# Products of the Fourier mode mixing moved from VectorE to GpSimd, with four buffers and another order of the data

## The reference, cut to what matters

```python
x = x + _L0_conv_ref(_gn(x), weight_re, weight_im, bias)
x = x + _L1_conv_ref(_gn(x), gamma, beta)

# _L0_conv_ref: 4 heads of 16 channels, the lowest 32 x 17 modes
x_freq = jnp.fft.rfft2(x, axes=(-2, -1))
xf = x_freq.reshape(B, 4, 16, fH, fW)
core = jnp.einsum('bhixy,hioxy->bhoxy', xf[:, :, :, :32, :17], weight)   # complex
out_freq = zeros.at[:, :, :, :32, :17].set(core)
x_out = jnp.fft.irfft2(out_freq, s=(H, W), axes=(-2, -1)) + bias
# _L1_conv_ref: a per-pixel normalization on the hyperboloid (arccosh, sqrt, a sum over channels)
```

## Time and profile before

| | |
|---|---|
| median of 3 runs | 4943.81 us (4943.03 to 4945.26) |
| span of the profiled execution | 4939.4 us |
| its own time | not given apart from the span; the median of the runs lies 4.4 us above the span |
| busy: PE, DVE, ACT, POOL | 77%, 69%, 45%, 30% |
| stage a, about | 0 to 1350 us |

### The profile page before, as it was taken

How to read it: one execution, slowest core, us unless ns; L and a number is a source line. 1 busy time by engine, 2 the same in 40 slices (tenths; PEclk the granted TensorE clock), 3 DMA queues, 4 the chain that set the end, 5 groups by cost and what they waited for, 6 DMA issues and landing times.

```text
span 4939.4 us, 72319 instructions
## 1 busy us (share of the span) xinstructions
PE 3805.1 (77%) x23619; PEld 2097.6 (42%) x23874; DVE 3399.5 (69%) x3499; ACT 2240.3 (45%) x3020; POOL 1460.1 (30%) x737
## 2 busy tenths in 40 slices
PE   7777777777144344433999999999999999999998
PEld 3444444444111011002555555555555555555554
DVE  2989889898863433343776677667767776676677
ACT  5555555455022233232554455445554554454544
POOL 0010110101100010001454444444444444444444
PEclk9988888898566677766999999999999999999999
DMA  9565756655099989982777777777777777777776
GB/s 367 192 251 188 258 198 229 228 193 213 14 381 357 364 342 363 351 345 81 224 235 219 227 239 221 224 223 241 224 222 224 237 227 224 227 234 224 223 244 217
DMA packets 288845, 1197.47 MB, mean 242 GB/s; under 512 B 30174, under 2 KB 46846, under 8 KB 205828
## 3 DMA queue, kind: packets, MB, share of 16 engines
q1 hardware_dynamic: 274740, 1151.85, 68.7%
q0 software_dynamic: 11600, 38.32, 2.1%
q10 hardware_dynamic: 2304, 4.20, 0.2%
HBM read 883.32 MB, written 310.94 MB: 242 GB/s over the span
## 4 chain that ended last, share of the span: by engine, by line
PE 50%; issue 3%; DMA 1%; DVE 0%; SPq 0%; POOL 0%; ACT 0%; POOLq 0%; ACTq 0%
PE c_p_u L1129 20%; PE c_p_z L1099 11%; PE c_p_t L1112 10%; PE c_p_p L1153 5%; PE c_p_g L1135 4%; DMA c_mv<-bmap 0%; POOL c_ot L1306 0%; ACT c_zc L1189 0%; DVE c_zc L1280 0%; DMA c_ys<-spec 0%; SPq L1070 0%; DMA c_x<-x 0%; DVE c_rt L1288 0%; SPq L1069 0%; PE c_p_z L1174 0%
## 5 line engine op out<-in xcount | busy, mean ns | idle before, releaser
L1306 POOL TENSOR_TENSOR c_ot<-c_s,c_u 128x1024 f32<-128x1024 f32 x512 | 1211.3, 2366 | 1411.6 <-DVE c_s L1259 1411.6
L1189 ACT ACTIVATE c_zc<-c_p_z 34x512 f32<-34x512 f32 x512 | 546.4, 1067 | 1316.0 <-PE c_p_z L1099 1261.5
L1250 DVE TENSOR_TENSOR c_u<-c_xt,c_p_u 128x1024 f32<-128x1024 f32 x512 | 625.3, 1221 | 745.0 <-PE c_p_u L1129 722.5
L1129 PE MATMUL c_p_u<-c_mv,c_zc 128*128 128x256 f32 x4096 | 1043.7, 399 | 76.5 <-issue 75.5
L1129 PEld LDWEIGHTS c_p_u<-c_mv,c_zc 128*128 128x128 f32 x4096 | 750.7, 193 | 590.1 <-issue 465.7
L650 PE MATMUL b_p_al<-b_xt,b_awc 128*32 128x512 f32 x2048 | 333.9, 791 | 502.6 <-ACT b_al_r L692 314.9
L1259 DVE SCALAR_TENSOR_TENSOR c_s<-c_u,keep_k,c_p_g 128x1024 f32<-128x1024 f32 x512 | 655.8, 1281 | 18.0
L1269 DVE TENSOR_TENSOR c_ot<-c_ot,c_p_p 128x1024 f32<-128x1024 f32 x512 | 621.4, 1214 | 1.8 <-POOL c_ot L1306 1.3
L1218 ACT ACTIVATE c_sq<-c_s,c_btcol 128x1024 f32<-128x1024 f32 x512 | 589.2, 1151 | 52.8 <-DVE c_s L1259 22.3
L1099 PEld LDWEIGHTS c_p_z<-c_idft_h,c_ys 128*34 128x34 f32 x8176 | 477.6, 113 | 224.7 <-issue 215.2
L1099 PE MATMUL c_p_z<-c_idft_h,c_ys 128*34 128x64 f32 x8176 | 559.6, 222 | 7.8 <-ACT c_zc L1189 7.8
(11 more groups left out here) (177 smaller groups left out, 3090.8 us busy)
## 6 DMA issues: line engine op xcount, KB each, us to landing
a_xt<-in_x SPq DMA_DIRECT2D x256, 1024.0 KB, 9.7
b_xt<-in_x SPq DMA_DIRECT2D x128, 2048.0 KB, 18.9
c_xt<-in_x SPq DMA_DIRECT2D x256, 1024.0 KB, 6.4
out<-c_ot SPq DMA_DIRECT2D x256, 1024.0 KB, 8.5
maps<-b_maps POOLq DMA_DIRECT2D x16, 768.0 KB, 14.9
c_rt<-maps SPq DMA_DIRECT2D x256, 48.0 KB
a_wm<-in_wmix SPq DMA_DIRECT2D x1, 8704.0 KB, 34.9
b_spt<-spec POOLq DMA_DIRECT2D x32, 272.0 KB, 23.4
```

The costliest lines, as they stand in the source:

```text
L1129: ins = nc.tensor.matmul(p_u[:, W * r:W * r + W], zc[ck % 2][:, (t % TCH) * ROWS + row], mv[t % 2][:, W * row:W * row + W], start=True, st ...
L1189: S.activation(zc[chunk_buffer][0:M2, :, 16 * part:16 * part + 16].rearrange("m h c -> m c h"), p_z[0:M2, :].rearrange("m (c h) -> m c h", ...
L1250: V.tensor_tensor(u[n][:], xt[t % 4][:, 1024 * n:1024 * n + 1024], p_u[:], ALU.add).then_inc(u_done, 1)
L1306: P.tensor_tensor(ot[t % 4][:, 1024 * n:1024 * n + 1024], s0[n][:], u[n][:], ALU.add).then_inc(v_done, 1)
```

## The change

GpSimd forms all the products of an image in `products(b)`: 16 of 128x1088, one for each output, into four buffers `prod` in turn. Each waits until the sum that last read its buffer is done (`y_sums`). `second_rstd(b-1)` and `store_stats(b-1)` stand behind the fourth product. VectorE's `mix(b, q)` keeps only the two reductions, each behind the semaphore of its product, and `mean_sum` is called behind the fourth `mix` of the next turn. `xh`, the weights and the products are laid out with ky outside and the 32 pairs (channel, real/imaginary part) innermost, so that a reduction reads neighbouring elements; `xh` is written with that permutation. The host lays the weights out in the same order.

```diff
+    NP = 4
-        xh = sb("xh", [128, CI, M2])
-        prod = [sb(f"prod{k}", [128, 2, CI * M2]) for k in range(2)]
+        xh = sb("xh", [128, KY, 2 * CI])
+        prod = [sb(f"prod{k}", [128, 2, CI * M2]) for k in range(NP)]
...
-            def mix(q, waited=None):
+            def mix(b, q, stored=None):
                 for o in (2 * q, 2 * q + 1):
-                    ch.inc(V.tensor_tensor(prod[o % 2][:], wm[:, o], xh[:].rearrange("p i m -> p (i m)").unsqueeze(1).to_broadcast((128, 2, CI * M2)), ALU.mult))
-                ch.wait()
-                for o in (2 * q, 2 * q + 1):
-                    if waited is not None and o == 0:
-                        dve.wait_ge(y_out, waited)
-                    ch.inc(V.tensor_reduce(y[:, o].rearrange("p (a k) -> p a k", a=2), prod[o % 2][:].rearrange("p a (n k) -> p a k n", k=KY), AX_X, ALU.add))
-                ch.wait()
+                    dve.wait_ge(prod_ready, b * CI + o + 1)
+                    if stored is not None and o == 0:
+                        dve.wait_ge(y_out, stored)
+                    V.tensor_reduce(y[:, o].rearrange("p (a k) -> p a k", a=2), prod[o % NP][:].rearrange("p a (k n) -> p a k n", k=KY), AX_X, ALU.add).then_inc(y_sums, 1)
             def finish(b):
+                dve.wait_ge(y_sums, b * CI + CI)
...
-                ch.inc(V.tensor_tensor(xh[:].rearrange("p (g i) m -> p g (i m)", i=2), xk[:].rearrange("p (g i) m -> p g (i m)", i=2),
-                                       row(22, 8).unsqueeze(2).to_broadcast((128, 8, 2 * M2)), ALU.mult))
+                ch.inc(V.tensor_tensor(xh[:].rearrange("p k (g j) -> p g j k", j=4), xk[:].rearrange("p i m -> p (i m)").rearrange("p (g j k) -> p g j k", j=4, k=KY),
+                                       row(22, 8).unsqueeze(2).unsqueeze(3).to_broadcast((128, 8, 4, KY)), ALU.mult))
...
-                dcs = pair(xh[:, :, 0])
-                ch.step(V.tensor_tensor(dcs, dcs, row(7, 8).unsqueeze(2).to_broadcast((128, 8, 2)), ALU.add))
-                if not is_at(b, 0):
-                    mean_sum(b - 1)
+                dcs = pair(xh[:, 0, 0::2])
+                V.tensor_tensor(dcs, dcs, row(7, 8).unsqueeze(2).to_broadcast((128, 8, 2)), ALU.add).then_inc(xh_ready, 1)
+                dve.wait_ge(xh_ready, b + 1)
...
-                    neg = wm[:, :, 0].rearrange("p o (i r k) -> p o i r k", r=2, k=KY)[:, :, :, 1]
+                    neg = wm[:, :, 0].rearrange("p o (n r) -> p o n r", r=2)[:, :, :, 1]
...
-                    mix(q, None if is_at(b, 1) or q else (b - 1) * 16)
+                    mix(b - 1, q, None if is_at(b, 1) or q else (b - 1) * 16)
+                    if q == 3 and not is_at(b, 1):
+                        mean_sum(b - 2)
...
+            def products(b):
+                pool.wait_ge(xh_ready, b + 1)
+                for o in range(CI):
+                    if not (is_at(b, 0) and o < NP):
+                        pool.wait_ge(y_sums, b * CI + o - NP + 1)
+                    P.tensor_tensor(prod[o % NP][:], wm[:, o], xh[:].rearrange("p k n -> p (k n)").unsqueeze(1).to_broadcast((128, 2, CI * M2)), ALU.mult).then_inc(prod_ready, 1)
+                    if o == 3 and not is_at(b, 0):
+                        second_rstd(b - 1)
+                        store_stats(b - 1)
...
+            products(0)
             with pool.Fori(1, B) as b:
                 first_rstd(b)
-                second_rstd(b - 1)
-                store_stats(b - 1)
+                products(b)
...
-PER_A = 63
+PER_A = 30
...
-    wmix = np.stack([np.stack([re, im], 4), np.stack([im, re], 4)], 3)
+    wmix = np.stack([np.stack([re, im], 4), np.stack([im, re], 4)], 3).transpose(0, 1, 2, 3, 6, 4, 5)
```

More of the change, by code:

```diff
@@ L161, in stage_a @@
     chain_end, macc_out, powers = sem("chain_end"), sem("macc_out"), sem("powers")
+    xh_ready, prod_ready, y_sums = sem("xh_ready"), sem("prod_ready"), sem("y_sums")
+    NP = 4
     with ExitStack() as mem:
@@ L502, in _ @@
             for q in range(Q):
-                mix(q, None if q else (B - 1) * 16)
+                mix(B - 1, q, None if q else (B - 1) * 16)
+                if q == 3:
+                    mean_sum(B - 2)
             finish(B - 1)
```

## The result

The changed kernel takes 4781.11 us (median of 4 runs, 4778.71 to 4782.78) against 4943.42 us (4 runs, 4935.26 to 4945.26): a ratio of 0.9674, 95% interval 0.966 to 0.9688, 162 us less. Forecast were 4680 us, a gain of 264. The direction was right and the time lies in the stated range (4650 to 4790), but above the bounds of the forecast case itself (4650 to 4710): 101 us of the gain did not come. The profiled execution has a span of 4777.1 us instead of 4939.4.

The account below looks back on a forecast made before the run. VectorE was taken to set the pace; afterwards GpSimd's and TensorE's chains would, at 61.2 us an image instead of 78.6. Saving 264 us from the 4939.4 us span, with 4.4 carried over, gave 4680 us; range 4650 to 4790.

Parts of the forecast that it names:

- the forecast case: The main case, chance 0.60: an image of 59.2 to 63 us, a total of 4650 to 4710.
- Part 1, the products: Multiplications move from VectorE to GpSimd: one product every 2.55 us, 40.8 us an image; bounds 2.37 and 3.7.
- Part 2, the reduction and xh: VectorE's contiguous reduction falls from 2.00 to 1.29 us; the strided write of xh costs +0.3 us an image.
- Part 3: Powers and store take 7.4 us between GpSimd's products 3 and 4; mean_sum loses its 4.3 us wait, keeps 0.5 us.
- the lock: Rival, chance 0.06: GpSimd and VectorE shut each other out of SBUF; 4.6 us a product, total 5192 us.
- Part 4, the sum for an image: Chains of GpSimd and TensorE counted from R, with a TensorE stall of 4.5 us: 61.2 us an image instead of 78.6.
- R: The last step of start(), when the normalized modes xh are ready; forecast to come every 61 us.
- First image, last image, tail: First image 55.9 us, last overlapped image 60.4, and the mixing after it 49.65.
- The edits at nothing: Weight sign flip, weight order in memory, the moved DMA queue wait and ScalarE's work were expected to cost nothing.
- The signs: Marks of being right: R every 61 us, products 2.5 to 2.6 apart, reduction 1.29, no energy wait, DMA above 260 GB/s.
- The dearer product: Rival, chance 0.16: GpSimd's product costs 3.0 us, an image 67.6 us, total 4782 us.

Follow-up runs that it names:

- e8_layout: The kernel before with the new order of the data alone, all products on VectorE: 4756.72 us.
- e1_moved: The changed kernel with mean_sum called behind the last pair of sums, in front of finish(): 4679.38 us.
- e2_two: e1_moved plus one addition of two unrelated 128x8 SBUF rows on VectorE behind the fourth pair of sums: 4781.92 us.
- e3_reduce: e1_moved plus one VectorE reduction of 128x16 to 128x8 behind the fourth pair of sums: 4674.78 us.
- e4_copy: e1_moved plus one fp32 128x8 copy from SBUF to SBUF on VectorE behind the fourth pair of sums: 4783.06 us.
- e5_np2: The changed kernel with 2 product buffers instead of 4: 4702.44 us.
- e12_allvector: The kernel before with the new order of the data and mean_sum behind the fourth pair of sums, all products on VectorE: 4695.43 us.

## Why the prediction was right, and where it was not

*Part 1, the products.* Forecast one every 2.55 us; measured 19.68/8 = 2.46, duration 2.50. The estimate from the Trainium skill (GPSIMD Engine Reference, section "Performance versus the Vector engine"), 2.39, lies below both by 0.07 and 0.11. By the prediction's own sum that estimate would lower the total by about 18 us and not 12: 12 for the thirteen images, and 2.6 each for the last one and the tail. The reductions slowed the products by about 1% at most (2.50 us in the median of all 256, 2.47 to 2.49 while line 433 waited and VectorE ran nothing else), and the products did not slow the reductions (1.28 us, as without them in e8_layout).

*Part 2, the reduction and xh.* Forecast 1.29 and +0.3; measured 1.28 and 1.11 - 0.725 = +0.39. Right.

*Part 3 is the step that failed.* It said of mean_sum: "its three short operations (0.5 us) stay". At its new place, inside GpSimd's run of products, the first of them took 8.57 us in place of 0.17. The term was sized by its duration at the old place, where GpSimd had no products. 13 x 8.0 us is the miss; e1_moved takes it away (4679 us) and e2_two brings it back (4782) with an unrelated instruction.

The prediction had the lock as a rival at 0.06 and rightly saw that reductions are the pair that no row covers. But it asked only whether the sixteen reductions contend with the products and never went through VectorE's other instructions between the first and the last product. It quoted the Trainium skill, SBUF — State Buffer, section "Who interferes with whom", which lists two SBUF inputs and two-port modes. By that rule mean_sum contends, since in `row(13, 8)` and `st[:, 0]` it has two SBUF inputs, and beside products the traces of e2_two, e3_reduce and e4_copy agree with the rule in all three cases. Trace and skill differ in the length. The skill has the lock held for one instruction. Here the wait went on over up to six products that followed each other; only in the first image did it end with the product then running.

They differ the other way as well, and the prediction was wrong that the trace of before had no pair to test the lock. It has one, GpSimd's power (two SBUF inputs) beside VectorE's copy to xk and its write of xh (two SBUF inputs), in fifteen images:

```profile
494.41 3.17 POOL L520 TENSOR_TENSOR a_st<-a_st,a_sm 128x16 f32<-128x16 f32 x1 [0.43 <-DVE a_st L429]
```

```profile
494.39 0.44 DVE L458 COPY a_xk<-a_xm 128x544 f32<-128x544 f32 x1
494.86 0.73 DVE L460 TENSOR_TENSOR a_xh<-a_xk,a_sm 128x544 f32<-128x544 f32 x1
```

The write of xh took 0.72 to 0.73 us beside the power, and 0.72 in the first image, where no power of line 520 runs yet. So VectorE was not shut out there; the power took 3.17 us beside VectorE and 2.93 the last time, without it. That GpSimd is busy is thus not enough: shutting out is shown for the products alone.

*Part 4, the sum for an image.* With mean_sum out of the products' way: 61.2 forecast, 61.45 measured in e1_moved, 4680 against 4679.38. The split within it was less good. TensorE's trace in e1_moved:

```profile
540.23 1.94 PE L263 MATMUL a_p_tr<-a_ident,a_rows 128*128 128x128 f32 x8 [3.21 <-DVE a_cols L376]
541.97 2.51 PE L275 MATMUL a_p_cols<-a_dft_w,a_cols 128*128 128x128 f32 x16
...
557.15 1.94 PE L263 MATMUL a_p_tr<-a_ident,a_rows 128*128 128x128 f32 x8 [2.70 <-DVE a_cols L376]
558.88 2.58 PE L275 MATMUL a_p_cols<-a_dft_w,a_cols 128*128 128x128 f32 x16
```

There are two stalls, of 3.2 and 2.7 us, and each is followed by a restart at the lower clock; the prediction had one of 4.5. Errors have cancelled in part, which is luck: with faster products the second restart came 24.1 us after R (533.04) and not 24.8, but it cost (1.94 - 1.09) + (2.58 - 1.95) = 1.5 us and not 0.65, and mean_sum's 0.5 us now stand in front of finish().

*First image, last image, tail*: 55.7, 61.3, 49.4 against 55.9, 60.4, 49.65. *The edits at nothing*: no row read here shows a cost of theirs; the loads ran at 245 GB/s in the changed kernel, and at 273 GB/s in e5_np2 (200 to 1000 us).

*The signs.* Of those that the prediction named for being right, the reduction came (1.28 us) and the wait for energy went. Others failed: R came every 69 us and not 61, products 2.46 us apart and not 2.5 to 2.6, TensorE's stall was 7.4 us and not 4 to 5, and the mean was 245 GB/s and not over 260.

*The rivals.* The dearer product gave 4782 us, which is what was measured, for a wrong reason: products took 2.50 us, not 3.0. The range was drawn up to 4790 for this rival, so it is luck that the measured time lies in it. A time that agrees does not confirm its mechanism. The lock was the right mechanism at another place: one VectorE instruction in an image waited for GpSimd, where the rival had each of the sixteen products wait for VectorE.

## What to carry to other kernels

When work moves to GpSimd, go through every instruction that VectorE runs between the first and the last of it, not only the ones that share its data: here an operation on two SBUF tiles or an fp32 copy within SBUF, of 8 elements a partition, waited in all images but the first until GpSimd paused, and more buffers put that pause off. Place such instructions where GpSimd has no such work, and look for the sign: a small instruction with a duration many times its usual one. And measure the parts of a change by themselves: here the order of the data alone (4757 us) beat the whole change, and e1_moved, with the products on GpSimd, is only 16 us faster than e12_allvector; with the powers moved too it is 75 us.

## What the runs showed of the hardware

- A small VectorE instruction with two SBUF inputs, or an fp32 copy within SBUF, of 128x8 elements took 8.57 us (median) beside GpSimd's products, a reduction of that size 0.16. In the rows shown it ends within 0.03 us of the end of GpSimd's run. The duration of such a row contains the wait; it is not listed as a wait.
- GpSimd kept VectorE out over all the products that it could run back to back: 3.70, 6.13, 8.57 and 13.43 us for 2, 3, 4 and 6 buffers. The exception is the first image of e2_two and e4_copy, 1.25 us; its reason is open.
- GpSimd's power of 128x16 did not keep VectorE out: in before the write of xh, with two SBUF inputs, took 0.72 to 0.73 us beside it and without it. The power took 3.17 us instead of 2.93.
- TensorE came back at the lower clock after stalls of 2.70 and 3.21 us in e1_moved: transposes of 1.94 us instead of 1.09.
- Reductions of 128x1088 on VectorE took 1.28 us beside products of 128x1088 on GpSimd and without them; the products stayed at 2.46 to 2.54 us.
